# A graph network on one Trainium2 core: the degree sums of an edge stage, made by GpSimd in place of VectorE

## The reference

```
src = edge_index[0]; dst = edge_index[1]
e_in = concatenate([x[src], x[dst]])
edge_new = relu(e_in @ We1 + be1) @ We2 + be2
agg = segment_sum(edge_new, dst)
```

## Time and profile before

| | |
|---|---|
| runs | 5278.63 us median of 3 (5277.78 to 5279.85) |
| profiled execution | 5283.64 us, its span 5281.8 us, mean granted TensorE clock 0.977 |
| TensorE busy over the span | 4941.9 us, 94% |
| VectorE busy | 4231.2 us, 80% |
| ScalarE busy | 3308.0 us, 63% |
| GpSimd busy | 1981.2 us, 38% |

### The profile page before, as it was taken

The page is one execution under the profiler, slowest core; times in us unless marked ns, Lnnn a source line. Parts: engine busy times, 40 slices in busy tenths (PEclk is TensorE's granted clock), DMA queues, the critical chain, the costliest instruction groups (busy, mean ns, idle before and its releaser), DMA issues. The chain is left out here.

```text
span 5281.8 us, 166491 instructions
## 1 busy us (share of the span) xinstructions
PE 4941.9 (94%) x56200; PEld 4423.4 (84%) x56200; DVE 4231.2 (80%) x7710; ACT 3308.0 (63%) x5897; POOL 1981.2 (38%) x2037
## 2 busy tenths in 40 slices
PE   5999989799999999999997879999999997899997
PEld 5888877699999999999997769999999997656655
DVE  7888862488888888888886669999999996688885
ACT  3555544477777777777774457777777774566651
POOL 3444437433333333333332655555555553300000
PEclk9999999899999999999998989999999998999988
DMA  4444421222222222222220133333333331000000
GB/s 169 176 161 171 168 100 67 92 98 96 93 101 93 98 93 96 94 101 96 94 96 29 50 109 132 130 127 131 132 128 128 130 132 35 1 0 0 0 0 25
DMA packets 199131, 498.18 MB, mean 94 GB/s; under 512 B 46467, under 2 KB 85366, under 8 KB 192630
## 3 DMA queue, kind: packets, MB, share of 16 engines
q1 hardware_dynamic: 190940, 490.58, 26.5%
q10 hardware_dynamic: 8090, 6.29, 0.4%
HBM read 466.49 MB, written 30.33 MB: 94 GB/s over the span
## 5 line engine op out<-in xcount | busy, mean ns | idle before, releaser
L1602 PE MATMUL ps<-kv_table,stage 128*128 128x256 bf16 x7203 | 892.5, 273 | 0.0
L1911 POOL TENSOR_TENSOR parts<-rest 128x512 bf16<-128x512 f32 x588 | 631.0, 1079 | 623.5 <-DVE rest L1970 617.1
L2109 PE MATMUL ps<-a_table,stage 128*128 128x128 bf16 x7203 | 795.1, 219 | 32.8 <-ACT stage L2041 32.8
L2112 PE MATMUL ps<-window,stage 128*128 128x128 bf16 x7350 | 812.5, 220 | 0.0
L1555 POOL TENSOR_TENSOR message<-message 128x512 f32<-128x512 f32 (+1 forms) x441 | 445.7, 1011 | 854.8 <-ACT message L1502 854.8
L1602 PEld LDWEIGHTS ps<-kv_table,stage 128*128 128x128 bf16 x7203 | 679.1, 98 | 68.0
L1419 DVE TENSOR_TENSOR product<-ps,q_kept 128x512 f32<-128x512 f32 (+1 forms) x637 | 426.8, 670 | 310.7 <-ACT message L1481 248.1
L2028 ACT ACTIVATE parts<-ps 128x512 bf16<-128x512 f32 x588 | 349.0, 594 | 330.3 <-PE ps L2112 327.1
L1591 PE MATMUL ps<-window,stage 128*128 128x128 bf16 x7350 | 515.9, 219 | 28.9 <-ACT stage L1495 28.7
L2109 PEld LDWEIGHTS ps<-a_table,stage 128*128 128x128 bf16 x7203 | 504.3, 98 | 35.5 <-issue 35.4
L2112 PEld LDWEIGHTS ps<-window,stage 128*128 128x128 bf16 x7350 | 514.6, 98 | 0.0
(11 more groups left out here) (368 smaller groups left out, 10686.1 us busy)
## 6 DMA issues: line engine op xcount, KB each, us to landing
stage<-lists SPq DMA_DIRECT2D x294, 768.0 KB, 4.1
edges<-in_edge_attr SPq DMA_DIRECT2D x49, 2240.0 KB, 8.5
stage<-lists SPq DMA_DIRECT2D x98, 896.0 KB, 5.4
window<-qkv_rows SPq DMA_DIRECT2D x49, 288.0 KB, 5.4
window<-ab_rows SPq DMA_DIRECT2D x49, 192.0 KB, 5.0
qkv_rows<-kv_table SPq DMA_DIRECT2D x21, 384.0 KB, 2.5
qkv_rows<-q_parts SPq DMA_DIRECT2D x21, 192.0 KB, 1.9
ab_rows<-a_table SPq DMA_DIRECT2D x21, 192.0 KB, 2.0
```

What stands on the lines that cost most here:

```text
L1602: last = nc.tensor.matmul(kv_ps[n % 2][:, i, :], from_src, kv_table[:, tile, q, :], start=(q == 0), stop=(q == 2))
L1911: pool.tensor_tensor(parts_of(n)[:, 0:nt, D:2 * D], rest[BUFFER[n]][:, 0:nt, :], middle[BUFFER[n]][:, 0:nt, :], ALU.subtract).then_inc(low ...
L2109: nc.tensor.matmul(to[:, i, :], from_src, a_table[:, tile, q, :], start=(q == 0), stop=False)
L2112: last = nc.tensor.matmul(to[:, i, :], own, window[d][:, (3 + q) * D:(4 + q) * D], start=False, stop=(q == 2))
```

## The change

`unit_degrees` moves from VectorE's program to GpSimd's. It waits for the same semaphores and makes the same two additions. On GpSimd it stands right behind `low_of` of batches 0, 3, 6 and 9. GpSimd waits once per round for the clearing of `degree_sum`, which VectorE still does, as it does the last fold. `unit_hots` keeps its wait for the sums of the unit two back.

```
                 @block.gpsimd
+                    def unit_degrees(j, u):
+                        first_tile, end = unit_tiles(u)[0], min(unit_tiles(u)[1], SELF)
+                        k = j * 4 + u
+                        pool.wait_ge(hots2, k + 3)
+                        pool.sem_inc(pool_waited, 1)
+                        folded = hots[u % 2][1][:, 0:(end - first_tile) * P].rearrange("p (t h s) -> p t h s", h=2, s=P // 2)
+                        for h in range(2):
+                            pool.wait_ge(degree2, 2 * k + h + 16)
+                            pool.sem_inc(pool_waited, 1)
+                            pool.tensor_tensor(degree_sum[:, first_tile:end, :], degree_sum[:, first_tile:end, :],
+                                               folded[:, :, h, :], ALU.add).then_inc(degree2, 1)
+
+                    def batch(j, n):
+                        low_of(j, n)
+                        if n % BATCHES in (0, 3, 6, 9):
+                            unit_degrees(j, n % BATCHES // 3)
+
                     with pool.Fori(0, total, NG) as first:
+                        pool.wait_ge(flushed2, first * 3 + (NG + 1))
+                        pool.sem_inc(pool_waited, 1)
                         with loop(pool, 0, HALF) as i:
                             for n in range(NB2):
-                                low_of(first + i * 2 + n // BATCHES, n)
+                                batch(first + i * 2 + n // BATCHES, n)
                         for n in range(BATCHES):
-                            low_of(first + (NG - 1), n)
+                            batch(first + (NG - 1), n)
                 @block.vector
-                    def unit_degrees(j, u):
-                        ... (the same, with dve for pool and without the sem_inc lines)
                             slots_of(j + d, g + d, n)
-                            if b in (0, 3, 6, 9):
-                                unit_degrees(j + d, b // 3)
                             if b in (1, 4):
                                 unit_hots(j + d, b // 3 + 2)
```

## The result

The changed kernel takes 5426.94 us (median; 5424.9 to 5431.46), the kernel before 5278.2 in the same comparison: ratio 1.0282, interval 1.0267 to 1.0297. It is 149 us slower; 5375 was forecast, with a range to 5455.

What follows compares the result with a forecast made beforehand. VectorE was taken to set the pace (26.73 us per group), TensorE right behind; GpSimd's terms summed to 28.7, and 1.97 us x 49 = +97 us on 5278.6 gave 5375 us, 63%, own range 5325 to 5450, 80% range 5250 to 5455.

Steps and rivals of the forecast that it cites:

- ceiling of 28 us: Stage layer2_edges: a VectorE of no cost brings a group only to TensorE's 26.16 us, 0.57 us x 49.
- The new bound: Stage layer2_edges: GpSimd becomes the bound at 28.7 us per group against 26.73, +97 us.
- 12.03 us: GpSimd's eight additions per group: 6 x 1.477 + 2 x 1.583 us, with bounds of 7.5 and 14.1.
- The line: GpSimd two-input instructions: 1.658 ns per column whatever the types, from rows of 512 (1.052 us) and 1750 columns (3.105).
- The dependent step: On GpSimd, a pair's second addition waits 0.19 us for the first; four per group, 0.76 us.
- The tolls: GpSimd time lent to VectorE at boundaries, per group: slot_hots 1.26 us, compares 1.08, counts 0.05.
- The wait for "rest": GpSimd's subtraction comes round before VectorE's "rest" after a group's last unit: 0.3 us per group (0 to 1).
- The compare's wait: VectorE's compare waits for degree sums on GpSimd; chain 6.53 us against GpSimd's 6.57, so counted at nothing.
- Rival A: GpSimd hides VectorE's passages under its start-up, 26.04 us; the group goes to TensorE's 26.16, -28 us, 5251; 13%.
- B: A second low part passes the compare at the boundary; queue behind it gives 31.7 us per group, +244, 5523; 8%.
- C: Full exclusion at the port: every VectorE passage costs GpSimd its whole duration, 33.9 us per group, +349, 5628; 5%.
- D: Additions on GpSimd cost 1.23 us each instead of 1.50; group stays 26.7 us, about 5279; 9%.

Runs made afterwards that it cites:

- quiet addition of 512: Changed kernel plus seven GpSimd instructions at the stage's end, other engines idle; this one is the degree addition at 512 columns: 1147 ns.
- kernels with one unit: Against the kernel before, only unit 1 of each group is summed by GpSimd, the other three by VectorE: 5319.91 us, ratio 1.0078.
- one addition of each unit on GpSimd: Against the kernel before: VectorE keeps each unit's first addition, GpSimd makes the second, compare one batch later: 5369.54 us, ratio 1.0174.
- two-unit kernels: Against the kernel before, GpSimd sums units 0 and 2, VectorE 1 and 3: 5326.94 us; the same with the compare one batch later: 5336.96 us.
- one moved line: Kernel before, both additions still on VectorE but issued one batch later, directly ahead of the compare: 5244.6 us, ratio 0.9934.

## Why the prediction was right or wrong

- The bound before: right. VectorE set the pace and TensorE was close behind. The ceiling of 28 us was too small; without additions the kernel gains 44 (5237.5 against 5281.6 in the same comparison), as TensorE's floor is 25.95 us, not 26.16. Busy time in a window was more than the engine needed.
- The new bound: right. GpSimd at 96%, TensorE waiting for its low parts, slot_hot's mean up from 0.45 to 0.93, the clock at 1.00. Halving only the additions' length took the whole loss away.
- The step that was mis-sized is the term "12.03 us" for the eight additions. They take 6 x 1.643 + 2 x 1.760 = 13.4 us on their own, 1.35 more per group, which is 66 us; the forecast was too low by 52, since smaller terms went the other way. The line was laid through rows of another form: the subtraction, whose operands are two views of one tile, and the product at line 281, with a broadcast operand. "Whatever the types" did not hold. The row taken for an outer bound was the right one: line 973 has two operands in different tiles, 1.154 us at 512 columns; the quiet addition of 512 took 1.147. The same line has 0.669 us at 256 columns in the trace of the kernel before, so it shows 1.89 ns per column, and 1.64 and 1.76 us for 768 and 832. With it the sum is 30.1 us and the forecast about 5440.
- The estimate by the Trainium skill, GPSIMD Engine Reference, section on performance against VectorE (2.2 ns per column, 13.8 us for the eight), was set aside for the rows' 1.66. The measured 1.88 lies between them, and the page's sum was the nearer one. Its figure is for f32; the one f32 instruction between two tiles here took 1.260 us for 512 columns.
- The dependent step, 0.19 forecast: 0.2. The tolls: 1.26 us per group forecast for slot_hot, 1.4 to 1.5 found by leaving it out; 1.13 forecast for the compares and counts, about 1.3 found. Right in size, a little low.
- The wait for "rest" was put at 0.3 us per group and came to 0.31. The compare's wait, counted at nothing, shows up only in this 0.31: issuing the compare later ended it, and gave no more.
- A term was left out of the sum: GpSimd's instructions overlap by about 0.04 us each where they follow one another (two subtractions, 2.35 us at 3723.29, and the next instruction starts at 3725.60). The durations of the 21 instructions of a group add up to 29.23 us, and the busy time is 28.61, 0.62 less. So 28.7 and 1.35 for the additions, 0.4 for the tolls, less 0.6 for the overlap and 0.2 for subtractions that alone take 1.04 and not 1.052, make the 29.7 that was measured. These smaller errors took 0.4 us off the 1.35, which is luck.
- Rival A (passages hidden, TensorE the bound) failed on the additions' length and on the tolls, which are not hidden. B failed: the compare got the first boundary (3716.02 to 3717.41), and issuing it later gave 15 us and not over 100. C, the lock at full price, is refuted: leaving out the 13 slot_hots gave about 1.4 us of GpSimd's time and not 5.3. The Trainium skill's rule (SBUF — State Buffer, shared port pair) names who waits, and the traces agree (0.62 against 1.40 us for one compare), but GpSimd lost less than what passed. D asked for additions of 1.23 us; they take 1.64.
- What the prediction did not see: that the same port makes the reverse direction costly. The kernels with one unit and with one addition of each unit on GpSimd show it. An addition that leaves VectorE frees 0.56 us of it (if it is the second of a pair), and takes the port for 1.64.

Open: how the loss of the two-unit kernels divides between VectorE's standing at the port (V), low parts that come late behind two additions (K), and ScalarE's later parts. TensorE stands there for low parts, and VectorE is idle 1.1 to 1.7 us per group for ScalarE (46.0 and 69.2 us in 1100); no run takes one away without the others.

## What to carry to other kernels

Moving an elementwise instruction from VectorE to GpSimd is not a matter of whose share is lower: before, look for VectorE instructions that get longer whenever GpSimd runs; each moved instruction shuts those out for its longer duration. Price the new instruction from a row with the same operand form (two tiles, one tile, broadcast, the types), and use that row for the sum, not for the bound. And read the standing out of the durations first: two instructions that each wait for the same port once can often stand together and wait once, which here gave 0.66% for one moved line.

## What the runs showed of the hardware

- A GpSimd two-input instruction costs 1.88 ns per column in bf16 between two tiles (667, 1147, 1631 ns at 256, 512, 768 columns), strided or not; 1467 instead of 1631 ns when one operand is broadcast; 1038 ns at 512 columns when the second operand is a bf16 view of the first one's f32 tile, 1154 for an f32 and a bf16 tile (line 973), 1260 between two f32 tiles.
- A VectorE slot_hot of 0.41 us (0.28 of it behind the boundary) that passes between two GpSimd instructions takes 0.1 to 0.2 us from GpSimd (1.4 to 1.5 us per group for 13 of them, 4 of which have a gap to pass in); a compare, 0.42 behind the boundary, about 0.3.
- Waiting at the port is booked as duration, on both engines: in the kernel before, VectorE showed 0.2 us of idle time per group, and yet about 0.8 us of standing in each of 8 instructions (1.39 against 0.56 us for the first and second addition of a pair, 1.40 against 0.62 for the compare). GpSimd's subtraction takes 1.04 us alone and 1.23 on average in the changed kernel. The same holds for the counts, 2 elements wide: 0.99 us, and 0.15 where it met no GpSimd instruction (one addition of each unit on either engine, at 3714.39).
